# Keys and values a stage earlier: a reordered pipeline in a gene-sum, attention and expert kernel

## What is computed

```python
h = einsum("bg,egp->bep", x, weight * mask) + bias   # 5000 genes, 16 positions
a = layernorm(h)
cq, ckv = layernorm(a @ W_dq), layernorm(a @ W_dkv)  # 64 and 85 wide
q, k, v = heads of cq @ W_uq, ckv @ W_ukv, with rotary parts; 8 heads of 16 + 2
h = h + causal_softmax(q k') v @ W_o.T
f = layernorm(h)
h = h + shared_ffn(f) + top2_of_64_experts_ffn(f)
```

## Time and profile before

| | us |
|---|---|
| median of 3 runs (242.53 to 243.67) | 243.42 |
| the profiled execution's own time | 243.9 |
| its span in the profile | 242.2 |
| PE busy | 184.0 (76%) |
| PE weight loads busy | 151.4 (63%) |
| DVE busy | 151.8 (63%) |
| POOL busy | 145.2 (60%) |
| ACT busy | 83.2 (34%) |

### The profile page before, as it was taken

The page is one execution under the profiler, slowest core; times in us unless marked ns, Lnnn a source line. Parts: engine busy times, 40 slices in busy tenths (PEclk is TensorE's granted clock), DMA queues, the critical chain, the costliest instruction groups (busy, mean ns, idle before and its releaser), DMA issues.

```text
span 242.2 us, 6074 instructions
## 1 busy us (share of the span) xinstructions
PE 184.0 (76%) x2479; PEld 151.4 (63%) x2479; DVE 151.8 (63%) x366; ACT 83.2 (34%) x245; POOL 145.2 (60%) x117
## 2 busy tenths in 40 slices
PE   0047967558989979979769669678999999999710
PEld 0046956456878968858658548455788778768410
DVE  0014385586487886897996976979876749101391
ACT  2005200003334323243152143346549764345500
POOL 3316469619998959979979949502054261176360
PEclk9999999977999989999999999955559999999965
DMA  6989999999999999999999999939801237433341
GB/s 210 285 295 421 353 414 395 334 422 415 420 414 416 423 420 420 413 426 418 407 389 221 216 217 200 145 91 306 229 1 34 84 104 210 142 100 89 110 98 47
DMA packets 32981, 65.11 MB, mean 269 GB/s; under 512 B 2874, under 2 KB 25367, under 8 KB 32375
## 3 DMA queue, kind: packets, MB, share of 16 engines
q1 hardware_dynamic: 31416, 59.47, 74.2%
q10 hardware_dynamic: 576, 3.26, 3.4%
q0 software_dynamic: 960, 1.97, 2.9%
HBM read 56.96 MB, written 7.73 MB: 267 GB/s over the span
## 4 chain that ended last, share of the span: by engine, by line
PE 41%; DVE 20%; DMA 11%; SPq 9%; ACT 8%; issue 5%; POOL 2%; POOLq 1%; ACTq 0%; DVEq 0%
PE bank L850 12%; DMA ring<-in_L_tok_weight_dram 9%; PE bank L1015 5%; DVE ring L1234 5%; SPq L370 4%; DVE bank L1262 4%; PE bank L1044 4%; DVE prod L1255 3%; PE bank L1027 2%; SPq L376 2%; PE bank L893 2%; PE bank L991 2%; PE bank L901 2%; PE bank L997 2%; DVE prod L1284 2%
## 5 line engine op out<-in xcount | busy, mean ns | idle before, releaser
L474 POOL TENSOR_TENSOR ring<-ring,mask 128x896 f32<-128x896 f32 (+1 forms) x48 | 91.6, 1935 | 19.6 <-DMA ring<-in_L_tok_weight_dram 19.5
L850 PE MATMUL bank<-ring,xT 128*64 128x128 f32 x1248 | 83.3, 291 | 12.3 <-DVE ring L1234 8.1
L850 PEld LDWEIGHTS bank<-ring,xT 128*64 128x64 f32 x1248 | 75.0, 147 | 17.6 <-DVE ring L1234 12.6
L1234 DVE TENSOR_TENSOR ring<-ring,bank 128x1024 f32<-128x1024 f32 (+1 forms) x45 | 45.7, 1048 | 36.0 <-DMA ring<-in_L_tok_weight_dram 36.0
L463 POOL TENSOR_TENSOR rstd<-mv,half 128x1 f32<-128x1 f32 (+1 forms) x24 | 14.3, 601 | 30.0 <-DVE mv L1242 23.1
L541 POOL DMA_INDIRECT ring<-expert_outputs,slot_index x16 | 16.1, 1003 | 16.7 <-DMA expert_outputs<-ring 12.5
L494 POOL DMA_INDIRECT expert_inputs<-xf,slot_index x14 | 14.3, 1022 | 5.9 <-DVE slot_index L1344 2.7
L831 PE MATMUL bank<-cst,w 64*128 64x64 f32 x39 | 5.3, 328 | 16.4 <-DMA w<-in_x_dram 15.7
L516 POOL TENSOR_TENSOR mask<-ring,mask 128x256 f32<-128x256 f32 x8 | 7.1, 890 | 17.0 <-ACT ring L711 17.0
L1015 PE MATMUL bank<-w,ring 128*64 128x128 f32 (+1 forms) x256 | 14.8, 296 | 0.6 <-ACT ring L711 0.6
L831 PEld LDWEIGHTS bank<-cst,w 64*128 64x128 f32 x39 | 5.0, 219 | 16.5 <-issue 15.7
(11 more groups left out here) (151 smaller groups left out, 294.0 us busy)
## 6 DMA issues: line engine op xcount, KB each, us to landing
ring<-in_L_tok_weight_dram SPq DMA_DIRECT2D x48, 832.0 KB, 13.0
expert_inputs<-w ACTq DMA_DIRECT2D x3, 1024.0 KB, 10.0
ring<-expert_inputs SPq DMA_DIRECT2D x6, 512.0 KB, 5.7
expert_outputs<-ring SPq DMA_DIRECT2D x12, 256.0 KB, 2.6
mask<-in_L_tok_mask_dram SPq DMA_DIRECT2D x3, 832.0 KB, 16.4
w<-in_x_dram SPq DMA_DIRECT2D x1, 1250.0 KB, 13.9
w2p<-in_L_ffn_w_dram SPq DMA_DIRECT2D x1, 1024.0 KB, 18.7
xT<-masks_dram SPq DMA_DIRECT2D x1, 1024.0 KB, 7.7
```

What stands on the lines that cost most here:

```text
L474: pool.tensor_tensor(unit(j, q, SPLIT(q // 2), UC), unit(j, q, SPLIT(q // 2), UC), mask[:, (m + SPLIT(q // 2)) * D:(m + UC) * D], ALU.mult ...
L850: last = pe.matmul(bank[0][64 * par:64 * par + 64, 0:D], xT[:, (UC * t + c) * B:(UC * t + c + 1) * B], unit(j, 2 * t + par, c, c + 1), sta ...
L1234: dve.tensor_tensor(both(j, t, a, b), both(j, t, a, b), m.rearrange("p (u f) -> p u f", u=1).to_broadcast([P, 2, (b - a) * D]), ALU.mult). ...
```

## The change

Nothing is computed differently; the lists of the five engines are written in another order. From stage 3 on, stage c projects pair a = c-1 (before c-2) while its own genes are summed; stage 2 projects pairs 0 and 1, one after the other. The heads that are made in stage c are still those of pair c-2, but their keys and values are ready from the stage before, so VectorE's stage is now `stats_h(a)`, `multiply_keys(b)`, `add_attended(d)`, three pieces, `choose(d)`, a piece, `place(d)`, `sum_scores(b)`, `less_max(b)`, a piece, `heads(b)`, a piece. The heads of pair 5 come into stage 7. The projection of pair 6 leaves the tail, which holds that of pair 7 alone; from `turn_o(k)`, `up(1)` on TensorE (k = 6) and `add_attended(k)` on VectorE the tail's order is as before.

The diff, without ScalarE's part (its list is put in the order of the chains above: `copy_oT(d)`, `norm_h(a)`, `norm_xf(d)`, `copy_xnT(a)`, `copy_xfT(d)`, `square_qk(a)`, `norm_qk(a)`, `turned_qk(a)`, `probs(b)`, `heads_k(a)`, `heads_v(a)`):

```diff
--- before.py
+++ after.py
@@ -54,8 +54,6 @@
 SCATTERED = {4: (0,), 5: (1,), 6: (2,), 7: (3,)}
 
 HELD = 4
-POOL_SHARE = (3, 3)
-VECTOR_SHARE = (2, 1, 2, 1)
 EPS = 1e-5
 NEG = -3.0e38
 SCALE = 1.0 / math.sqrt(DK)
@@ -496,15 +494,25 @@
                         in_=xf[:, j, :], in_offset=None, bounds_check=ROWS[j // NCH1] - 1, oob_is_err=False).then_inc(s_scat[j // NCH1], 16)
 
             for c in range(NCH):
-                b, d = c - 2, c - 3
-                mask_pieces(POOL_SHARE[0])
-                if d >= 0:
+                a, d = c - 1, c - 3
+                if c < 2:
+                    mask_pieces(UNITS)
+                    if c == 1:
+                        root_h(0)
+                elif c == 2:
+                    mask_pieces(2)
+                    root_qk(0)
+                    root_h(1)
+                    mask_pieces(3)
+                    root_qk(1)
+                    mask_pieces(1)
+                else:
+                    mask_pieces(2)
+                    root_h(a)
                     root_h2(d)
-                if b >= 0:
-                    root_qk(b)
-                mask_pieces(POOL_SHARE[1])
-                if c >= 1:
-                    root_h(c - 1)
+                    mask_pieces(2)
+                    root_qk(a)
+                    mask_pieces(2)
                 for j in SCATTERED.get(c, ()):
                     scatter(j)
 
@@ -518,10 +526,9 @@
             scatter(NCH1 - 1)
             pool.wait_ge(s_pmask, UNITS * NCH)
             j, k, l = NCH - 3, NCH - 2, NCH - 1
-            root_qk(k)
             root_h(l)
+            root_h2(j)
             root_qk(l)
-            root_h2(j)
             mid(0)
             mid(1)
             root_h2(k)
...
@@ -942,40 +955,49 @@
                     pe.wait_ge(s_rope, 2)
                     pe.wait_ge(s_qw, 16 * 6)
                     pe.wait_ge(s_centred, 2)
-                project_b, attend_d = b >= 0, d >= 0
                 ahead = 2 if c >= SUMS_AHEAD else 0
                 for n in range(ahead):
                     sum_genes(c, n)
-                if attend_d:
+                if c == 2:
+                    turn_xn(0)
+                    project(0)
+                if d >= 0:
                     turn_o(d)
-                if project_b:
-                    turn_xn(b)
-                if attend_d:
                     attend(d)
-                if project_b:
-                    project(b)
                 for n in range(ahead, 4):
                     sum_genes(c, n)
-                if attend_d:
+                if c == 2:
+                    turn_qk(0)
+                sum_genes(c, 4)
+                if c == 2:
+                    qkv(0)
+                    sum_genes(c, 5)
+                    values(0)
+                if a >= 1:
+                    turn_xn(a)
+                if d >= 0:
                     turn_xf(d)
-                if project_b:
-                    turn_qk(b)
-                sum_genes(c, 4)
-                if attend_d:
+                if a >= 1:
+                    project(a)
+                if d >= 0:
                     gate(d)
-                if project_b:
-                    qkv(b)
-                if attend_d:
+                for n in range(6 if c == 2 else 5, 8):
+                    sum_genes(c, n)
+                if d >= 0:
                     rank_tokens(d)
-                sum_genes(c, 5)
-                if project_b:
-                    values(b)
-                for n in range(6, 12):
-                    sum_genes(c, n)
-                    if c == NCH - 1 and n == 10:
-                        turn_xn(c - 1)
-                if c == NCH - 1:
-                    project(c - 1)
+                sum_genes(c, 8)
+                if c == 2:
+                    sum_genes(c, 9)
+                if a >= 1:
+                    turn_qk(a)
+                if c != 2:
+                    sum_genes(c, 9)
+                if a >= 1:
+                    qkv(a)
+                sum_genes(c, 10)
+                if a >= 1:
+                    values(a)
+                sum_genes(c, 11)
 
             def turn_xs(g):
                 if g % 2 == 0:
@@ -1064,21 +1086,18 @@
                 last.then_inc(s_sh2, 1)
 
             j, k, l = NCH - 3, NCH - 2, NCH - 1
-            turn_qk(k)
-            qkv(k)
+            turn_o(j)
+            attend(j)
             turn_xn(l)
-            turn_o(j)
             project(l)
-            values(k)
-            attend(j)
+            turn_xf(j)
+            turn_qk(l)
+            gate(j)
+            qkv(l)
             turn_xs(0)
-            turn_qk(l)
+            values(l)
             turn_xs(1)
-            qkv(l)
-            turn_xf(j)
             up(0)
-            gate(j)
-            values(l)
             turn_xs(2)
             turn_o(k)
             up(1)
@@ -1358,32 +1377,41 @@
 
 
                 a, b, d = c - 1, c - 2, c - 3
-                mask_pieces(VECTOR_SHARE[0])
-                if d >= 0:
-                    add_attended(d)
                 if c == 1:
+                    mask_pieces(2)
                     turn_rope()
                     centre_projections()
-                mask_pieces(VECTOR_SHARE[1])
+                    mask_pieces(1)
+                    stats_h(0)
+                    mask_pieces(3)
+                    continue
                 if c == 0:
+                    mask_pieces(3)
                     dve.wait_ge(s_rem, 32)
                     dve.wait_ge(s_mrem, 16)
                     dve.tensor_tensor(wrem[0:GREM], wrem[0:GREM],
                                       mrem[0:GREM, :].rearrange("p (a n) -> p a n", a=1).to_broadcast([GREM, S, D]),
                                       ALU.mult).then_inc(s_remm, 1)
-                mask_pieces(VECTOR_SHARE[2])
-                if d >= 0:
+                    mask_pieces(3)
+                    continue
+                stats_h(a)
+                if c == 2:
+                    mask_pieces(3)
+                    multiply_keys(b)
+                else:
+                    multiply_keys(b)
+                    add_attended(d)
+                    mask_pieces(3)
                     choose(d)
-                if a >= 0:
-                    stats_h(a)
+                mask_pieces(1)
                 if d >= 0:
                     place(d)
-                if b >= 0:
-                    scores(b)
-                    less_max(b)
-                mask_pieces(VECTOR_SHARE[3])
-                if b >= 0 and c < NCH - 1:
-                    heads(b)
+                sum_scores(b)
+                less_max(b)
+                mask_pieces(1)
+                heads(b)
+                mask_pieces(1)
+
             def shared_mid(i):
                 dve.wait_ge(s_ssil, i + 1)
                 if i == 1:
@@ -1422,17 +1450,15 @@
                                          ALU.mult, ALU.add).then_inc(s_fin, 1)
 
             j, k, l = NCH - 3, NCH - 2, NCH - 1
-            weigh_values(j)
             stats_h(l)
-            weights(0, NCH1)
-            sum_heads(j)
             multiply_keys(k)
+            add_attended(j)
             sum_scores(k)
             less_max(k)
-            add_attended(j)
             weigh_values(k)
             sum_heads(k)
             choose(j)
+            weights(0, NCH1)
             multiply_keys(l)
             add_attended(k)
             sum_scores(l)
```

More of the change, by code:

```diff
@@ L678, in _ @@
                     copy_oT(d)
-                if b >= 0:
-                    copy_xnT(b)
-                    square_qk(b)
+                if c == 1:
+                    norm_h(0)
+                if c == 2:
+                    copy_xnT(0)
+                    square_qk(0)
+                    norm_qk(0)
+                    turned_qk(0)
+                    heads_k(0)
+                    heads_v(0)
+                if a >= 1:
+                    norm_h(a)
                 if d >= 0:
                     norm_xf(d)
-                if b >= 0:
-                    norm_qk(b)
+                if a >= 1:
+                    copy_xnT(a)
                 if d >= 0:
                     copy_xfT(d)
-                if b >= 0:
-                    copy_qkv(b)
-                if c == NCH - 1:
-                    norm_h(a)
-                    copy_xnT(a)
-                if b >= 0:
+                if a >= 1:
+                    square_qk(a)
+                if c == 2:
+                    probs(0)
+                if a >= 1:
+                    norm_qk(a)
+                    turned_qk(a)
+                if b >= 1:
                     probs(b)
-                if 0 <= a < NCH - 2:
-                    norm_h(a)
+                if a >= 1:
+                    heads_k(a)
+                    heads_v(a)
             def copy_xsT(g):
@@ L734, in _ @@
             keep_h(l)
-            square_qk(k)
-            score_exp(0, NCH1)
-            norm_qk(k)
-            turned_qk(k)
-            norm_h(l)
-            heads_k(k)
```

(23 more changed lines are left out.)

3 lines of the change are left out of this document (1 added, 2 removed).

## The result

The changed kernel takes 255.74 us in the median of 4 runs (254.66 to 258.98) against 243.14 for the kernel before on the same chip: a ratio of 1.0504, 95% interval 1.0457 to 1.0551. It is slower by 5%; 254.3 was forecast. The profiled execution spans 254.0 us, 11.8 more than before.

A forecast was written before the change was run, and what follows sets the result against it. VectorE was taken to pace the stages, with a chain as the tail. A 4.2, B 7.75, C -4.2 and D 3.1 made +10.85 on 243.9, less 0.5: 254.3 us, range 243.0 to 258.5.

The forecast's parts named there:

- part D: Tail, pair 5's heads to pair 6 attended: pair 7's root held by key products, turns reordered; +3.1 us.
- signs that were named: `place` instruction over 1 us in stages 3 to 7, rank wait about 1.3 us, tail stretch 21 us.
- A: Stage 2 carries two chains, pair 1's behind pair 0's values: lag 5.2 us there, 4.2 after stage 3.
- part B: Stages 3 to 7: `place` instructions with two SBUF inputs held by GpSimd's units, 1.55 us a stage, 7.75 in all.
- C: Stages 3 to 7, heads to heads: waits of 9.9 us go, rank waits of 6.3 come, work -0.6; together -4.2.
- Rival 3: TensorE's clock drops in stages 3 to 7 too, 1 us a stage in four stages, giving 258.3 us; chance 0.12.

The follow-up runs named there:

- Pair 0 in stage 1: Changed kernel with pair 0's projection, keys and values made in stage 1, so stage 2 carries pair 1's chain alone; 250.65 us, 1.0409 of the kernel before.
- the early rank: Changed kernel with `rank_tokens(d)` on TensorE moved between quarters 5 and 6 of the sums; 248.62 us, 1.0322 of the kernel before.

## Why the prediction was right, and where its parts were not

The sign and the sum held: 10.9 forecast, 11.8 in the profile. The mechanism of each part was there, but the sizes erred both ways and nearly cancelled: up to pair 1's heads the lag was 3.6 us more than forecast, from there to pair 5's heads 0.5 less, in part D 1.6 less and behind it 0.6 less. That the sum came so near is in part luck. Of the signs that were named, some did not come: `place` was held for over 1 us in stages 3, 4 and 6 only, the rank was waited for 3.0 us a stage and not 1.3, and part D's stretch took 19.7 us and not 21.

**A, too small.** Forecast 5.2 at the end of stage 2, measured 7.7. All steps came within 0.5 us except one: projection to `turn_qk`, 2.94 taken from the tail's start, where nothing stands between; in stage 2 60 sums do, 4.55 us, the first of them at a granted clock of 0.50 (69 to 71 us). The queries were ready at 71.5 and TensorE came to them at 73.8. Pair 0 in stage 1 shows that this lag is paid nearly in full. Stage 3 took 17.0 us against 15.4 before; without its 2.8 us of holding, which belong to part B, that is the 14.2 of the forecast.

**B, right in kind, too large.** 5.1 us were held, not 7.75, because the rank came later than assumed and `place` so missed the units in stages 5 and 7. From the second third's end to L1360 1.9 us were assumed; it took 2.5 to 2.6 us in stages 3, 4 and 6, where L1360 was held, and 3.4 and 4.3 us in stages 5 and 7, where it came when the last unit was all but through or past it. That the holding is paid in full was part of the forecast. Stage 3 without it bears that out (2.4 of 2.8 us less, with 0.4 of longer instructions), and so does the sum of the early rank. The runs that took it away were not faster, but they paid some 2 us in the tail, so they don't show that it was free; what its removal alone would give in time was not measured.

**C, too small a wait.** 6.3 forecast for the ranks of stages 4 to 7, 12.1 measured. Quarters 6 and 7 were costed at 0.8 us, and that is the step that failed; they are 28 products, 1.75 at full clock and up to 3.3 at half. The earlier trace rows would have given 1.65 (28 of the 52 sums in 3.06 us). Rival 3 had the clock, but as a mean of 1 us a stage, not at this place. The same term stands in the 1.9 us of part B, so it made C's wait too small and B's holding too large at once. B and C together, from pair 1's heads to pair 5's, were to be +2.0 and were +1.5: B's share 2.2 instead of 6.2, the rest -0.7 instead of -4.2. The early rank shows that the late rank cost about 6 us.

**D, right at the front.** The root was held for 2.21 us and `qkv` came 9.3 us behind the heads (9.7 forecast). Behind it I forecast 11.6, and 10.4 were measured; so the part came to +1.5 and not +3.1. What the root's holding costs in time was below what could be told.

The Trainium skill (SBUF — State Buffer, section "Who interferes with whom") also says that `tensor_scalar` with one SBUF input can enter a mode that takes both ports. I had not used that; the held TENSOR_SCALAR of 128x2 (0.93 us) and of 128x64 (3.17 us for two) agree with it.

## What to carry to other kernels

When a chain is moved ahead, count what stands between its steps in each engine's own list, at the clock of that place: a step's latency from another stage, with nothing between, is only a lower bound. A rank, gate or other small result that VectorE waits for should be put on TensorE ahead of the sums that wait for another engine, if it doesn't depend on them. Count the sums themselves from a row, at both levels of the clock. And before an effect is called worthless because taking it away gains nothing, look for what the edit costs at every place that it reaches: here `place` without holding gained 2.4 us in stage 3 and lost 2.0 in the tail, where nothing had been held. A plan that took the late rank, the second chain and the holding away together came out 1.2% ahead of the kernel before.

## What the runs showed of the hardware

- Beside GpSimd's mask units, a TENSOR_SCALAR on one SBUF tensor of 128x2 float32 took 0.93 us, and two of 128x64 took 3.17; the same operation on 128x1 with a per-partition scalar took 0.20 to 0.21 in all stages, three of them (3, 5 and 6) beside a unit. What decides between them was not varied further.
- The holding goes both ways: a root of 0.55 on GpSimd took 2.21 beside VectorE's products of two SBUF tensors and 0.56 when one of them was in PSUM.
- Products put into some 1.5 us of TensorE's idle time in four stages, and into a fifth where 0.16 us were idle, kept the 28 products behind them at full clock (1.75 us). The granted clock was 0.50 behind another gap instead, and the kernel became 7 to 8 us slower.
- Behind the same wait of 1.5 us those 28 products ran at a granted clock of 1.00, 0.67 and 0.51 in three stages of one execution.
